# Graph network kernel: VectorE picks a gathered row by halving the candidates, with ScalarE copying the first half out of PSUM

## The chip, the cores and the metric

The kernel runs on one core of a Trainium2 chip. The metric is the device time of one execution in microseconds (us). Before the change three runs gave 5144.82, 5143.08 and 5143.58 us, median 5143.58.

## The reference, cut to what matters

```python
w = relu(edgefeats @ fnet_w1 + fnet_b1) @ fnet_w2 + fnet_b2      # 400000 edges, 13 -> 32 -> 256
W = w.reshape(-1, 16, 16)
for _ in range(2):                                               # NREPEATS
    xj = hx[edge_src]                                            # a row of 16 numbers for each edge
    m = einsum('ei,eio->eo', xj, W)
    agg = segment_sum(m, edge_dst, num_segments=12500) * inv_deg[:, None]
    hx = gru_cell(agg, hx, ...)
out = layernorm(x + hx)
```

The change concerns `hx[edge_src]`, the gather of 400000 rows out of a table of 12500, done twice. Everything else is as before.

## The kernel before, in words

The edges are sorted by destination. They are cut into tiles of 128 edges, one for each partition, and 64 tiles make a super-tile (a super, below). There are 49 supers (NSUP) in each of two rounds (`rnd` 0 and 1). Each super is worked in eight steps (`k`, HPS = 8) of eight tiles. Every engine runs its own program, written out by hand in its order, and meets the others at semaphores. A super has its number `s` in the round; `sup` counts through both rounds.

**Two ways to gather.** In each step of eight tiles POOL fetches five (six in step 0 of round 0) by indirect DMAs (line 535), and TensorE gathers the last three (two there) for the super that comes next. The numbers stand in BY_PE (line 33). POOL may be up to three steps ahead of the products (LEAD, line 532).

**The gather on TensorE.** The table is held in SBUF as `parts`: partition p and block kb hold 25 consecutive rows of 16 numbers (AR = 25, KB = 4), split into a high and a low part. ScalarE makes the one-hot matrix `src_hot` from the edges' block numbers: for each kb an absolute difference (`src_hots`, line 603), then one Relu over all four (line 607). TensorE multiplies it with the parts (`gather_rows`, line 722, 8 matmuls a tile, 24 for three tiles) into one of three PSUM banks `ps_g[j]`. After that each edge has 25 candidate rows, 400 numbers, in PSUM, of which one is its own.

**The pick on VectorE.** `rows_hot` (line 1125) writes once for each super `at_hot`, a one-hot of length 25 for each edge. `pick_rows` (line 1137) multiplies the 400 candidates of a tile by it, from PSUM into the SBUF tile `picked`, and raises `s_picked`, which frees the bank. `keep_rows` (line 1145) sums the 25 candidates of a step's tiles in one reduction of 1200 elements into `xg`, where the gathered rows of all tiles come together.

**The order of the work.** In step k of a super TensorE does `products` (line 732, 16 matmul records), in round 0 `hidden` for the next super (line 709), then what belongs to the step: in step 0 the `aggregate` of the super before (line 755, 32 records) behind some `own_sums` (line 745), in step 2 `turn` (line 762), in steps 4 and 5 `scatter` (line 776). At the end of the step stands `gather_rows` for step k of the next super. It waits for `s_src_hot` and for the pick of the tile that had the bank before (`slot_free`).

ScalarE in step 0 does `src_hots` of step 0 of the next super, `keep_agg` (line 582, waits for the aggregate), `keep_products` (line 576), in round 0 `relu` (line 570), and then `src_hots` of step 1. In steps 1 to 6 it begins with `src_hots` of step k + 1, which waits until the gather of step k - 1 is through, because there are two buffers of `src_hot`. Then come `keep_products` and `relu`. Step 7 has no `src_hots`.

VectorE in step k does `spread` (line 1092, the product of `xg` with the destination's one-hot, which TensorE's `products` of the same step waits for), `one_hot` and `keep_hot` (lines 1080 and 1100), in some steps `add_windows` (line 1165) and `keep_own` (lines 1115 and 1119), then the picks and the reduction for the gather of step k - 1, and once a super `places` (line 1151) and `rows_hot`.

## Time and profile before

| | us |
|---|---|
| median of three runs | 5143.58 |
| span of the profiled execution | 6694.6 |
| TensorE matmuls busy in it | 5648.0 (84%) |
| VectorE busy | 4296.9 (64%) |
| POOL busy | 3811.1 (57%) |
| ScalarE busy | 3179.0 (47%) |

The times are those of unrecorded runs; no time other than its span is given for the profiled execution, which is 1551 us longer than the median. The profile counts an instruction as busy from its start to its end, and neighbours on an engine may overlap. The ends of matmuls are modelled. Idle time stands with what ended it: "issue" where the profile shows nothing that was waited for, "remote" where the release came from something it can't name.

### The profile page before, as it was taken

To read this page: it belongs to the slowest core of one execution; us is meant where nothing else is said; L and a number is where in the kernel's file an instruction comes from. 1 tells how busy PE (TensorE), PEld (TensorE's weight loads), DVE (VectorE), ACT (ScalarE), POOL (GpSimd) and SP (SyncE) were. 2 spreads that over 40 slices of the span, in tenths; PEclk is the share of its full clock that TensorE was granted. 3 is DMA by queue.
4 is the path that set the end of the run, shared out by engine and by line. 5 is a ranking of instruction groups with operands and counts; after the bars stand their busy time and mean duration, and the time that the engine had idled before them with its cause. 6 is when DMAs were issued, how large, how long until landed. Compare 5 with 4: busy or idle time off the path is not lost.

```text
span 6694.6 us, 119595 instructions
## 1 busy us (share of the span) xinstructions
PE 5648.0 (84%) x38360; PEld 4666.6 (70%) x38361; DVE 4296.9 (64%) x7146; ACT 3179.0 (47%) x5259; POOL 3811.1 (57%) x4021
## 2 busy tenths in 40 slices
PE   2888888888888888888858888888888888888887
PEld 1777777777777777777647777776777777777775
DVE  3766666666666666666636666666666666666665
ACT  1554555445554545454325454454545454444442
POOL 6355555555555555555555555555555555555553
PEclk7988998889898999998878898898988889888887
DMA  4111111111111111111111111111111111111110
GB/s 107 46 34 48 34 48 34 48 34 48 34 48 44 39 48 34 48 34 48 25 47 29 40 29 40 33 37 39 31 40 29 40 29 41 29 40 29 40 29 20
DMA packets 197656, 263.32 MB, mean 39 GB/s; under 512 B 95745, under 2 KB 165942, under 8 KB 184205
## 3 DMA queue, kind: packets, MB, share of 16 engines
q1 hardware_dynamic: 61885, 216.66, 9.5%
q0 software_dynamic: 128192, 33.07, 4.8%
q10 hardware_dynamic: 7026, 6.21, 0.4%
q8 instruction: 348, 5.70, 0.4%
q14 instruction: 205, 1.68, 0.1%
HBM read 195.73 MB, written 54.92 MB: 37 GB/s over the span
## 4 chain that ended last, share of the span: by engine, by line
PE 65%; issue 14%; another core or an unknown queue 10%; ACT 6%; DVE 3%; DVEq 1%; DMA 0%; POOL 0%; ACTq 0%; POOLq 0%; SPq 0%
PE ps_all L722 45%; PE ps_all L732 8%; ACT src_hot L603 3%; PE ps_all L755 3%; PE ps_all L745 3%; PE ps_all L709 3%; PE ps_all L776 2%; ACT src_hot L607 2%; DVE shared L1137 1%; DVE fan L1092 1%; PE ps_all L762 0%; ACT shared L576 0%; ACT h_sb L570 0%; DVE xg L1145 0%
## 5 line engine op out<-in xcount | busy, mean ns | idle before, releaser
L722 PE MATMUL ps_all<-parts,src_hot 125*128 125x400 f32 x18048 | 3820.4, 368 | 258.7 <-issue 166.4
L722 PEld LDWEIGHTS ps_all<-parts,src_hot 125*128 125x128 f32 x18048 | 3501.9, 202 | 482.6 <-issue 367.7
L535 POOL DMA_INDIRECT xg<-in_x,idx x2027 | 1923.4, 949 | 1394.3 <-issue 556.1
L535 POOL DMA_INDIRECT xg<-h_rows,idx x1979 | 1873.1, 946 | 1371.6 <-issue 518.7
L1137 DVE TENSOR_TENSOR shared<-ps_all,at_hot 128x400 f32<-128x400 f32 x2256 | 1211.8, 566 | 1858.8 <-remote 1168.4
L603 ACT ACTIVATE src_hot<-keys,neg_key 128x384 fp32r<-128x384 int16 (+1 forms) x3072 | 1617.0, 599 | 1653.1 <-remote 979.0
L732 PE MATMUL ps_all<-fan,h_sb 128*32 128x160 f32 x12544 | 825.0, 316 | 489.5 <-issue 435.8
L1092 DVE TENSOR_TENSOR fan<-xg,ps_all 128x1280 f32<-128x1280 f32 x784 | 1158.8, 1478 | 88.0 <-DVE xg L1145 33.4
L607 ACT ACTIVATE src_hot<-src_hot 128x1536 fp32r<-128x1536 f32 (+1 forms) x768 | 1122.2, 1461 | 72.3 <-ACT src_hot L603 2.8
L1145 DVE TENSOR_REDUCE xg<-shared 128x48 f32<-128x1200 f32 (+1 forms) x768 | 1056.7, 1376 | 75.6 <-DVE shared L1137 1.0
L732 PEld LDWEIGHTS ps_all<-fan,h_sb 128*32 128x32 f32 x12544 | 391.8, 111 | 842.4 <-issue 794.9
L576 ACT COPY shared<-ps_all 128x320 f32<-128x320 f32 x784 | 330.2, 421 | 638.1 <-remote 431.2
L582 ACT COPY agg_sb<-ps_all 128x160 f32<-128x160 f32 x98 | 28.7, 293 | 981.0 <-remote 630.7
L755 PE MATMUL ps_all<-shared,w2s 128*64 128x160 f32 x3136 | 328.9, 349 | 70.3 <-issue 69.3
L745 PE MATMUL ps_all<-xg,shared 128*80 128x136 f32 (+1 forms) x1568 | 323.0, 317 | 75.1 <-issue 58.7
L709 PE MATMUL ps_all<-w_sb,ef 105*128 105x264 f32 x784 | 314.5, 483 | 66.5 <-issue 43.9
L745 PEld LDWEIGHTS ps_all<-xg,shared 128*80 128x80 f32 x1568 | 223.5, 168 | 193.1 <-issue 150.3
L755 PEld LDWEIGHTS ps_all<-shared,w2s 128*64 128x64 f32 x3136 | 259.3, 161 | 126.5 <-issue 117.6
L1165 DVE TENSOR_TENSOR acc_all<-acc_all,ps_all 33x144 f32 (+1 forms) x384 | 114.1, 297 | 236.3 <-remote 174.3
L709 PEld LDWEIGHTS ps_all<-w_sb,ef 105*128 105x128 f32 x784 | 131.0, 207 | 191.1 <-issue 179.4
L776 PE MATMUL ps_all<-place,agg_t 80*33 80x144 f32 (+1 forms) x1568 | 189.6, 336 | 64.0 <-issue 60.4
L1115 DVE TENSOR_TENSOR shared<-ps_all,mask 80x256 f32<-80x256 f32 (+3 forms) x490 | 180.4, 368 | 42.1 <-remote 20.4
(120 smaller groups left out, 1383.7 us busy)
## 6 DMA issues: line engine op xcount, KB each, us to landing
keys<-key_d SPq DMA_DIRECT2D x96, 768.0 KB
h_d<-h_sb SPq DMA_DIRECT2D x49, 1056.0 KB
h_sb<-h_d SPq DMA_DIRECT2D x49, 1056.0 KB
xg<-in_x,idx POOLq DMA_INDIRECT x2027
xg<-h_rows,idx POOLq DMA_INDIRECT x1979
ef<-in_ef_t SPq DMA_DIRECT2D x49, 420.0 KB
acc_all<-agg_t SPq DMA_DIRECT2D x1, 3161.0 KB
idx<-in_src_tiles SPq DMA_DIRECT2D x98, 32.0 KB
```

What stands on the lines that cost most here:

```text
L535: pool.indirect_dma_start(out=xg[:, buf, at, 0:C], out_offset=None, in_=rows_of, in_offset=bass.IndirectOffsetOnAxis(ap=idx[:, buf, at:at ...
L576: act.copy(pev[:, :, 2 * k:2 * k + 2, :].rearrange("p i u n -> p u i n"), ps_p[k % 2][:, 0:2 * C * WIN].rearrange("p (u i n) -> p u i n", ...
L603: act.activation(src_hot[:, k % 2, kb, 0:some * P], keys[:, buf, first * P:(first + some) * P], ACT.Abs, bias=neg_key[:, kb:kb + 1]).then_ ...
L607: act.activation(hot_of, hot_of.bitcast(F32), ACT.Relu, bias=1.0, scale=-1.0).then_inc(s_src_hot, some)
L709: pe.matmul(ps_h[:, 0:HT * HA], ef[:, buf, k, :], w1_sb[:], start=True, stop=True).then_inc(s_h, 1)
L722: last = pe.matmul(ps_g[j], src_hot[0:KP, k % 2, kb, j * P:(j + 1) * P], parts[0:KP, m, kb, :], start=(kb == 0 and m == 0), stop=(kb == KB ...
L732: last = pe.matmul(ps_p[k % 2][b * HID:(b + 1) * HID, u * C * WIN:(u + 1) * C * WIN], h_sb[:, buf, k * HT + u * BPS + b, 0:HID], fan[:, k ...
L745: last = pe.matmul(ps_own[n][:, u, 0:TQ * ca], hot_sb[:, j, b].rearrange("p t n -> p (t n)"), xg[:, buf].rearrange("p (j t b) c -> p j b t ...
L755: last = pe.matmul(ps_agg[lo:lo + BPS * C, 0:TPB * WIN], w2s[:, i, :], pev[:, i].rearrange("p t n -> p (t n)"), start=(i < 2), stop=(i >= ...
L1092: dve.tensor_tensor(fan[:, k % 2], xg[:, buf, k * HT:(k + 1) * HT, 0:C].unsqueeze(3).to_broadcast([P, HT, C, WIN]), hot[:, k % 2].unsqueez ...
L1137: dve.tensor_tensor(picked[:, j], ps_g[j].rearrange("p (a c) -> p c a", a=AR), at_hot[:, u].unsqueeze(1).to_broadcast([P, C, AR]), ALU.mul ...
L1145: dve.tensor_reduce(xg[:, buf, at:at + many, 0:C], picked[:, 0:many], AX_X, ALU.add).then_inc(s_xg_pe, many)
```

## The change

The 25 candidates are halved twice. NEAR is 13 and FEW is 7. ScalarE copies the first 13 candidates of a tile (208 numbers) from PSUM to the SBUF tile `near_rows`. VectorE overlays the other 12 (192 numbers) from PSUM by a predicated copy, in those edges whose row lies in the second half (`is_far[:, 0]`). It then overlays candidates 7 to 12 on 0 to 5 for a whole step's tiles (288 numbers), where `is_far[:, 1]` says so. It multiplies seven candidates by a one-hot of length 7 (336 numbers for three tiles) and sums them (336 numbers).

```diff
+NEAR = (AR + 1) // 2
+FEW = (NEAR + 1) // 2
...
+            def near_half(rnd, s, k):
+
+                wait_pos(act, s_cut, pe_count(rnd, s, pe_tiles(rnd, k)[0][0]))
+                for j, (n, _, _) in enumerate(pe_tiles(rnd, k)):
+                    act.wait_ge(s_g, pe_count(rnd, s, n) + 1)
+                    act.copy(near_rows[:, j].rearrange("p a c -> p (a c)"), ps_g[j][:, 0:NEAR * C]).then_inc(s_near, 1)
...
                     for k in range(HPS):
+                        if k > 0 and not is_last(i):
+                            near_half(rnd, 2 * i + par + 1, k - 1)
+                        elif k == 0 and not is_first(i, par):
+                            near_half(rnd, 2 * i + par, HPS - 1)
                         if k == 0 and not is_last(i):
                             src_hots(rnd, i + par, 1 - par, 2 * i + par + 1, 0)
...
             def rows_hot(rnd, s):
 
-                wait_pos(dve, s_picked, pe_count(rnd, s, 0))
-                dve.tensor_tensor(at_hot[:], iota_ps[:, 0:AR].unsqueeze(1).to_broadcast([P, TG, AR]),
-                                  at_pe[:, bass.ds(s * TG, TG)].unsqueeze(2).to_broadcast([P, TG, AR]),
+                mine = bass.ds(s * TG, TG)
+                wait_pos(dve, s_cut, pe_count(rnd, s, 0))
+                dve.tensor_tensor(at_hot[:], iota_ps[:, 0:FEW].unsqueeze(1).to_broadcast([P, TG, FEW]),
+                                  at_pe[:, mine].unsqueeze(2).to_broadcast([P, TG, FEW]),
                                   ALU.is_equal).then_inc(s_at_hot, 1)
+                dve.tensor_scalar(is_far[:, 0], at_side[:, mine], 2.0, None, ALU.is_ge).then_inc(s_at_hot, 1)
+                dve.wait_ge(s_at_hot, 3 * (rnd * (NSUP - 1) + s) - 1)
+                dve.scalar_tensor_tensor(out=is_far[:, 1], in0=is_far[:, 0], scalar=-2.0, in1=at_side[:, mine],
+                                         op0=ALU.mult, op1=ALU.add).then_inc(s_at_hot, 1)
...
                         if n == 0:
-                            dve.wait_ge(s_at_hot, rnd * (NSUP - 1) + s)
-                        dve.wait_ge(s_g, pe_count(rnd, s, n) + 1)
-                        wait_pos(dve, s_xg_pe, pe_count(rnd, s, n - j))
-                        dve.tensor_tensor(picked[:, j], ps_g[j].rearrange("p (a c) -> p c a", a=AR),
-                                          at_hot[:, u].unsqueeze(1).to_broadcast([P, C, AR]),
-                                          ALU.mult).then_inc(s_picked, 1)
+                            dve.wait_ge(s_at_hot, 3 * (rnd * (NSUP - 1) + s))
+                            dve.nop(nofuse=True)
+                        dve.wait_ge(s_near, pe_count(rnd, s, n) + 1)
+                        dve.nop(nofuse=True)
+                        dve.copy_predicated(near_rows[:, j, 0:AR - NEAR, :],
+                                            is_far[:, 0, u:u + 1].unsqueeze(2).to_broadcast([P, AR - NEAR, C]),
+                                            ps_g[j][:, NEAR * C:AR * C].rearrange("p (a c) -> p a c", c=C)).then_inc(
+                                                s_picked, 1)
...
             def keep_rows(rnd, s, buf, k):
...
                 dve.wait_ge(s_picked, pe_count(rnd, s, n) + many)
-                dve.tensor_reduce(xg[:, buf, at:at + many, 0:C], picked[:, 0:many], AX_X,
+                dve.nop(nofuse=True)
+                dve.copy_predicated(near_rows[:, 0:many, 0:NEAR - FEW, :],
+                                    is_far[:, 1, u:u + many].unsqueeze(2).unsqueeze(3).to_broadcast(
+                                        [P, many, NEAR - FEW, C]),
+                                    near_rows[:, 0:many, FEW:NEAR, :]).then_inc(s_few, many)
+                dve.wait_ge(s_few, pe_count(rnd, s, n) + many)
+                wait_pos(dve, s_xg_pe, pe_count(rnd, s, n))
+                dve.tensor_tensor(few_rows[:, 0:many], near_rows[:, 0:many, 0:FEW, :].rearrange("p m a c -> p m c a"),
+                                  at_hot[:, u:u + many].unsqueeze(2).to_broadcast([P, many, C, FEW]),
+                                  ALU.mult).then_inc(s_cut, many)
+                dve.wait_ge(s_cut, pe_count(rnd, s, n) + many)
+                dve.tensor_reduce(xg[:, buf, at:at + many, 0:C], few_rows[:, 0:many], AX_X,
                                   ALU.add).then_inc(s_xg_pe, many)
```

In the first super VectorE works out `at_pe` and the new `at_side` for all tiles once; four more small operations over 1176 columns and a drain are added there (`columns_of_tiles`).

On ScalarE the rows at the start of a super in round 0 (step 0, then the beginning of step 1) read so before; line 603 and 607 are `src_hots`, 582 `keep_agg`, 576 `keep_products`, 570 `relu`:

```order
L603 ACTIVATE src_hot<-keys,neg_key 128x256 [waits s_g,s_keys0]
L603 ACTIVATE src_hot<-keys,neg_key 128x256 x3
L607 ACTIVATE src_hot<-src_hot 128x4x256 [waits s_src_far]
L582 COPY agg_sb<-ps_all 128x160 [waits s_agg]
L576 COPY shared<-ps_all 128x2x16x10 [waits s_p]
L570 ACTIVATE h_sb<-ps_all 128x264 [waits s_h,s_h_out0]
L603 ACTIVATE src_hot<-keys,neg_key 128x384 [waits s_g]
L603 ACTIVATE src_hot<-keys,neg_key 128x384 x3
L607 ACTIVATE src_hot<-src_hot 128x1536 [waits s_src_far]
L603 ACTIVATE src_hot<-keys,neg_key 128x384 [waits s_g]
```

In the changed kernel the same stretch is these rows (line 611 and 615 are `src_hots`, 622 is the new copy of the near half; its lines are those of the changed kernel):

```order
L622 COPY shared<-ps_all 128x208 [waits s_g,s_cut]
L622 COPY shared<-ps_all 128x208 [waits s_g] x2
L611 ACTIVATE src_hot<-keys,neg_key 128x256 [waits s_g,s_keys0]
L611 ACTIVATE src_hot<-keys,neg_key 128x256 x3
L615 ACTIVATE src_hot<-src_hot 128x4x256 [waits s_src_far]
L590 COPY agg_sb<-ps_all 128x160 [waits s_agg]
L584 COPY shared<-ps_all 128x2x16x10 [waits s_p]
L578 ACTIVATE h_sb<-ps_all 128x264 [waits s_h,s_h_out0]
L611 ACTIVATE src_hot<-keys,neg_key 128x384 [waits s_g]
L611 ACTIVATE src_hot<-keys,neg_key 128x384 x3
L615 ACTIVATE src_hot<-src_hot 128x1536 [waits s_src_far]
L622 COPY shared<-ps_all 128x208 [waits s_g,s_cut]
L622 COPY shared<-ps_all 128x208 [waits s_g]
L611 ACTIVATE src_hot<-keys,neg_key 128x384 [waits s_g]
```

So three copies that wait for the gather of step 7 now stand ahead of the first `src_hots` of a super, and the copies of the gather of step 0 stand behind the `src_hots` of step 1.

On VectorE step 4 of a super read so before; the first three rows are `spread`, `one_hot` and `keep_hot`, the last two the picks and the reduction for the gather of step 3:

```order
L1092 TENSOR_TENSOR fan<-xg,ps_all 128x1280 [waits s_xg0_4,s_xg_pe,s_p,s_hot]
L1080 TENSOR_TENSOR ps_all<-ps_all,rel 128x80 [waits s_hot_sb]
L1100 COPY shared<-ps_all 128x2x4x10
L1137 TENSOR_TENSOR shared<-ps_all,at_hot 128x400 [waits s_xg_pe,s_g] x3
L1145 TENSOR_REDUCE xg<-shared 128x3x16 [waits s_picked]
```

Now they are:

```order
L1120 TENSOR_TENSOR fan<-xg,ps_all 128x1280 [waits s_xg0_4,s_xg_pe,s_p,s_hot]
L1108 TENSOR_TENSOR ps_all<-ps_all,rel 128x80 [waits s_hot_sb]
L1128 COPY shared<-ps_all 128x2x4x10
L1171 COPY_PREDICATED shared<-is_far,ps_all 128x192 [waits s_near] x3
L1181 COPY_PREDICATED shared<-is_far,shared 128x3x96 [waits s_picked]
L1187 TENSOR_TENSOR shared<-shared,at_hot 128x336 [waits s_xg_pe,s_few]
L1191 TENSOR_REDUCE xg<-shared 128x3x16 [waits s_cut]
```

The pick no longer waits for TensorE but for ScalarE's copy (`s_near`), and four operations became six, the last four of them in a chain.

## Rows read from the trace of the kernel before

**Rows 1.** The page: span, busy shares, and the chain that ended last by engine.
```profile
span 6694.6 us, 119595 instructions
...
PE 5648.0 (84%) x38360; PEld 4666.6 (70%) x38361; DVE 4296.9 (64%) x7146; ACT 3179.0 (47%) x5259; POOL 3811.1 (57%) x4021
...
PE 65%; issue 14%; another core or an unknown queue 10%; ACT 6%; DVE 3%; DVEq 1%; DMA 0%; POOL 0%; ACTq 0%; POOLq 0%; SPq 0%
```

**Rows 2.** Groups of matmuls: count | busy us, mean ns of one | idle before.
```profile
L722 PE MATMUL ps_all<-parts,src_hot 125*128 125x400 f32 x18048 | 3820.4, 368 | 258.7 <-issue 166.4 <-ACT src_hot L607 74.4 <-DVE shared L1137 11.0
...
L732 PE MATMUL ps_all<-fan,h_sb 128*32 128x160 f32 x12544 | 825.0, 316 | 489.5 <-issue 435.8 <-DVE fan L1092 48.6 <-ACT h_sb L570 2.8
...
L755 PE MATMUL ps_all<-shared,w2s 128*64 128x160 f32 x3136 | 328.9, 349 | 70.3 <-issue 69.3
L709 PE MATMUL ps_all<-w_sb,ef 105*128 105x264 f32 x784 | 314.5, 483 | 66.5 <-issue 43.9 <-DMA ef<-in_ef_t 18.8 <-ACT h_sb L570 2.4
...
L745 PE MATMUL ps_all<-xg,shared 128*80 128x136 f32 (+1 forms) x1568 | 323.0, 317 | 75.1 <-issue 58.7
```

**Rows 3.** The chain in order of time, 2236 to 2260: start, us, what.
```profile
2237.04 0.68 PE ps_all L732 x16
2237.72 0.64 PE ps_all L709 x2
2238.37 4.37 PE ps_all L722 x24
...
2244.06 0.47 PE ps_all L745 x4
...
2246.30 1.83 PE ps_all L755 x22
```

**Rows 4.** Busy time of each engine in a stretch; third from the right: granted clock.
```profile
2237.00:2249.00 12.00, 11.34 (x102) 9.55 (x102) 8.73 (x12) 4.21 (x11) 6.38 (x8) 1.00 0.55 182
```

**Rows 5.** Groups of VectorE and ScalarE.
```profile
L1137 DVE TENSOR_TENSOR shared<-ps_all,at_hot 128x400 f32<-128x400 f32 x2256 | 1211.8, 566 | 1858.8 <-remote 1168.4 <-PE ps_all L722 506.7 <-issue 180.3
...
L1145 DVE TENSOR_REDUCE xg<-shared 128x48 f32<-128x1200 f32 x720 | 1010.0, 1403 | 75.5 <-DVE shared L1137 1.0 <-issue 0.5
...
L576 ACT COPY shared<-ps_all 128x320 f32<-128x320 f32 x784 | 330.2, 421 | 638.1 <-remote 431.2 <-PE ps_all L732 179.2 <-issue 25.5
...
L1080 DVE TENSOR_TENSOR ps_all<-ps_all,rel 128x80 f32<-128x80 f32 x784 | 189.2, 241 | 0.2 <-issue 0.2
...
L582 ACT COPY agg_sb<-ps_all 128x160 f32<-128x160 f32 x98 | 28.7, 293 | 981.0 <-remote 630.7 <-PE ps_all L755 313.9 <-issue 36.4
```

**Rows 6.** Instructions in order of time, round 1, from a gather's end (start, us).
```profile
5027.67 0.57 DVE L1137 TENSOR_TENSOR shared<-ps_all,at_hot 128x400 f32<-128x400 f32 x1 [0.88 <-PE ps_all L722]
...
5028.35 1.40 DVE L1145 TENSOR_REDUCE xg<-shared 128x48 f32<-128x1200 f32 x1
...
5032.63 1.04 DVE L1137 TENSOR_TENSOR shared<-ps_all,at_hot 128x400 f32<-128x400 f32 x2
```

**Rows 7.** The same, round 0, from the end of an aggregate to the gather of step 1.
```profile
2248.17 0.29 ACT L582 COPY agg_sb<-ps_all 128x160 f32<-128x160 f32 x1 [6.22 <-PE ps_all L755]
...
2248.47 0.95 POOL L535 DMA_INDIRECT xg<-in_x,idx  x1 [0.30 <-issue]
...
2248.96 2.13 ACT L603 ACTIVATE src_hot<-keys,neg_key 128x384 fp32r<-128x384 int16 x4
...
2251.19 1.48 ACT L607 ACTIVATE src_hot<-src_hot 128x1536 fp32r<-128x1536 f32 x1
...
2252.72 1.72 PE L722 MATMUL ps_all<-parts,src_hot 125*128 125x400 f32 x8 [0.16 <-issue]
```

**Rows 8.** The same place in round 1.
```profile
3643.16 0.29 ACT L582 COPY agg_sb<-ps_all 128x160 f32<-128x160 f32 x1 [12.13 <-PE ps_all L755]
...
3645.90 1.49 ACT L607 ACTIVATE src_hot<-src_hot 128x1536 fp32r<-128x1536 f32 x1
...
3648.36 2.81 PE L722 MATMUL ps_all<-parts,src_hot 125*128 125x400 f32 x14
```

More of the change, by code:

```diff
@@ L175, in gnn_program @@
         near_tmp, far_tmp = (shared[:, lo:lo + CHUNK * TPB] for lo in (3920, 4120))
-        picked = shared[:, 4320:4320 + 3 * C * AR].rearrange("p (m c a) -> p m c a", m=3, a=AR)
+        near_rows = shared[:, 4320:4320 + 3 * C * NEAR].rearrange("p (m a c) -> p m a c", m=3, a=NEAR)
+        few_rows = shared[:, 4320 + 3 * C * NEAR:4320 + 3 * C * (NEAR + FEW)].rearrange("p (m c a) -> p m c a", m=3, a=FEW)
         agg_sb = sb("agg_sb", [P, TPB * WIN])
@@ L194, in gnn_program @@
         keys = sb("keys", [P, 2, TG * P], I16)
-        at_pe = sb("at_pe", [P, NSUP * TG])
+        at_pe = sb("at_pe", [P, NSUP * TG], I16)
         parts = sb("parts", [P, PARTS, KB, AR * C], F32R)
@@ L198, in gnn_program @@
         neg_key = sb("neg_key", [P, KB])
-        at_hot = sb("at_hot", [P, TG, AR])
+        at_hot = sb("at_hot", [P, TG, FEW])
+        at_side = sb("at_side", [P, NSUP * TG], I16)
+        is_far = sb("is_far", [P, 2, TG], U32)
         stat_all = sb("stat_all", [P, 2, GROUPS, RJ])
@@ L293, in gnn_program @@
         s_g = sem("s_g")
+        s_near = sem("s_near")
         s_picked = sem("s_picked")
+        s_few = sem("s_few")
+        s_cut = sem("s_cut")
         s_xg_pe = sem("s_xg_pe")
@@ L1050, in columns_of_tiles @@
                 key_of(key_col, src_col, whole_col)
-                dve.tensor_tensor(at_pe[:], src_col.bitcast(I32), key_col, ALU.subtract).then_inc(s_staged, 1)
+                link(dve.tensor_tensor(key_col, src_col.bitcast(I32), key_col, ALU.subtract))
+                link(dve.tensor_scalar(whole_col, key_col, float(NEAR) - 0.5, None, ALU.is_ge))
+                link(dve.scalar_tensor_tensor(out=key_col, in0=whole_col, scalar=-float(NEAR), in1=key_col,
+                                              op0=ALU.mult, op1=ALU.add))
+                link(dve.tensor_scalar(src_col, key_col, float(FEW) - 0.5, None, ALU.is_ge))
+                dve.scalar_tensor_tensor(out=at_side[:], in0=whole_col, scalar=2.0, in1=src_col,
+                                         op0=ALU.mult, op1=ALU.add)
+                dve.scalar_tensor_tensor(out=at_pe[:], in0=src_col, scalar=-float(FEW), in1=key_col,
+                                         op0=ALU.mult, op1=ALU.add)
+                dve.drain().then_inc(s_staged, 1)
                 dve.wait_ge(s_staged, 1)
```

6 lines of the change are left out of this document (3 added, 3 removed).

## The prediction

> **What bounds the kernel now.** I read the page first. TensorE is busy 84% of the recorded span, VectorE 64%, POOL 57%, ScalarE 47%, and the chain of work that ended last runs 65% through TensorE and 3% through VectorE [rows 1]. The reader is to see that the engine which the change relieves is hardly in that chain.
>
> A busy TensorE is not TensorE at its peak, so I next asked for the pieces of that chain in order of time, in a stretch whose granted clock is 1.00, the level of 2.4 GHz [rows 3, 4]. There 24 gather matmuls take 4.37 us, 16 records of products 0.68, two of hidden 0.64, four of own sums 0.47, and 22 of the aggregate 1.83, so 32 of them 2.66 [rows 3]. With the counts of the groups [rows 2]: 18048/24 = 752 gathers are 3286 us, 784 products 533, 392 hidden 251, 392 fours of own sums 184, 98 aggregates 261. That is 4515 us, 88% of the median of 5143.6. The other 628 us must hold the scatters, the turns, the head, the gate stages of two rounds and all stalls. So in unrecorded runs TensorE works nearly without a pause. The recorded span of 6694.6 is 1551 us longer; the idle time that the groups put down to "issue" and "remote" [rows 2, 5] is where it went, since the medians leave no room for it. I therefore count a change's cost in the stretches without stalls, add it to the recorded execution's own time and to the median alike, and trust no wait that stands as "remote".
>
> Then the picks. VectorE's 2256 picks had 1858.8 us of idle time before them, and none of that is VectorE's own work [rows 5]; in a clean step the pick of the third tile starts the moment the gather is over [rows 6]. The gather in turn waited for a pick only 11.0 us in all [rows 2]. VectorE follows TensorE; it doesn't hold it up.
>
> **The change, part by part.**
>
> *VectorE's work.* A line through 80 elements at 241 ns and 400 at 566 [rows 5] has 1.02 ns an element and 160 ns fixed. By it 192 elements are 355 ns, 288 are 452, 336 are 501. Before, three picks in a row start 0.47 apart (two take 1.04), then 0.11 of wait, then 1.40 of reduction: 2 x 0.47 + 0.57 + 0.11 + 1.40 = 3.02 us a step [rows 6]. Now it is 2 x 0.26 + 0.355 + 0.11 + 0.452 + 0.11 + 0.501 + 0.11 + 0.501 = 2.66. That is 0.36 less a step, 271 us over 752 steps. It is far less than the element count promises (1536 against 2400), because six fixed parts and four waits stand where there were four and two. From the third tile on nothing is won: 2.08 before, 2.14 now. None of this is on the path while TensorE is the bound, so I take 0 for it.
>
> The predicated copy stands nowhere in the trace. It can't be shorter than the row of 80 elements, 241 ns; if it needs two passes an element, 192 elements are 0.55 and 288 are 0.75, and a step gets 0.9 longer. I take one pass, as all VectorE rows here; both ends go into the range.
>
> The row shows 160 ns fixed in each VectorE instruction [rows 5]. The Trainium skill ("VectorE: DVE Perf Modes", section on the TRN2 errata) speaks against this change: sources in SBUF pay a fixed latency per instruction, so one should keep tiles at 512 elements or more, and here all four new kinds are below. Its table (120 cycles plus the elements from PSUM, 58 from SBUF, at 0.96 GHz) would make a step 0.78 shorter, where the rows make it 0.36; as neither is on the path, the forecast would be the same.
>
> *`rows_hot`.* 600 elements become 168 (by the line 0.77 and 0.33 us), and two operations of 24 elements with a wait come in (2 x 0.18 + 0.11): nothing. *`columns_of_tiles`* adds four operations of 1176 elements, 1.36 each, once, 5 us. They lie in the first super, where POOL fetches all 64 tiles at 1.25 us each (0.95 and 0.30 of issue [rows 7]), 80 us. I take 0; without that cover it would be 5.
>
> *ScalarE's work.* Copies of 160 and 320 numbers from PSUM take 293 and 421 ns [rows 5], so 208 take 331. 2256 of them are 747 us; ScalarE's 3179 become 3926, 76% of the median. The work fits, but the queue is in order, and its order decides at the start of each super.
>
> *Step 1, round 0.* Before, the gather of step 1 started at 2252.72, 0.05 after the one-hot of step 1 was ready (2251.19 + 1.48) [rows 7]: here ScalarE is already what TensorE waits for, last of all. Now the near halves of step 0 stand behind that one-hot, and the gather needs the bank of tile 0, which is free only after ScalarE's copy and VectorE's overlay. From the one-hot's end: 0.05 + 0.33, 0.10 until VectorE starts, 0.355, 0.05. That is 0.89 where it was 0.05, so 0.84 us more in each of 48 supers: **+40 us**.
>
> *Step 1, round 1.* The one-hot was ready at 3647.39 and the gather came only at 3648.36, since TensorE had more of its own to do [rows 8]. 0.89 later is 3648.28: it just fits, 0.
>
> *Step 0.* The three copies for step 7 now stand ahead of the first one-hot of a super. From the end of the gather of step 7: 0.05 + 0.33 + 0.05, then 3.71 for the one-hot (from 2248.96 to 2252.67 [rows 7]), 4.14 in all. TensorE meanwhile has products, own sums and aggregate, 0.68 + 0.47 + 2.66 = 3.81 [rows 3]. In round 1 the gather of step 0 so comes 0.33 to 0.39 late, and 0.39 x 48 = **+19 us**. In round 0 there is hidden too (0.64), and the one-hot is only two tiles wide: 0. Before, this one-hot was made while the gather of step 7 still ran.
>
> *Other steps.* ScalarE now has 3 x 0.33 + 3.71 + 0.42 + 0.38 + 0.1 = 5.6 in a step of round 0, TensorE 0.68 + 0.64 + 4.37 = 5.69; in round 1 it is 5.2 against 5.05. A backlog of 0.15 in a bare step is worked off in the steps with own sums, turn or scatter. I take 0. Queued behind the new waits for `s_g` are the one-hots, which waited for the same gather anyway.
>
> The sum is 40 + 19 = 59 us: 5143.6 + 59 = **5203 us** (the recorded span by the same sum 6754).
>
> **The rivals.**
>
> *VectorE does hold TensorE up in unrecorded runs*, in steps 5 to 7, where the window sums and own sums come on top and the fan is late. Then 0.36 is won in 3 steps of 96 supers, 104 us, and with the 59 the time is 5099. It decides once VectorE's slack in those steps is below the 0.36. For it: the sum of TensorE's pieces leaves some stalls open. Against it: 11.0 us of waits for picks [rows 2]. Chance 0.20.
>
> *POOL sets the pace.* 41 fetches at 1.25 us are 51 us a super, and 5143.6/98 is 52.5. Then a stall of 0.84 on TensorE falls into a wait that is there anyway, and nothing changes: 5144. Against it: the fetches' spacing would leave no room for the gate stages. Chance 0.15.
>
> *ScalarE becomes the bound.* If each copy costs 0.44, as the copies that wait for TensorE do (0.42 for 320 numbers), a step has 0.33 more, 0.2 over TensorE in round 0 and 0.45 in round 1, in the four steps that have nothing added: 48 x 4 x 0.65 = 125, and 5328. Chance 0.10.
>
> *The halving doesn't shorten VectorE's work*, because the predicated copy takes two passes: 0.9 - 0.36 = 0.54 more a step, late in three steps of eight: 96 x 3 x 0.54 = 156 and the 59 make 5358. Chance 0.05.
>
> **How the numbers follow.** My forecast has 0.50; with the last two slower is 0.65. A measurement of this kernel can tell about 0.2%, 10 us, from no change; the POOL case is the 0.15 for that, the VectorE case the 0.20 for faster. The range goes from 5085, a little under the VectorE case, to 5310, which takes in the forecast with half the backlog cost and leaves out most of the last two.
>
> **What would show it.** In the profile after: VectorE's busy time down by some 250 us and ScalarE's up by some 750; the predicated copies near 355 and 452 ns; in round 0 the gather of step 1 some 0.9 us behind the end of the one-hot of step 1 instead of 0.05; in round 1 the first gather of a super right behind its one-hot, which ends after the aggregate. Idle time before the gathers that is put down to VectorE's picks, 11.0 us now, should grow by tens of us. It is wrong if the time falls: then VectorE's work was on the path in unrecorded runs although the trace doesn't show it; or if nothing moves, then the start of a super has slack that I don't see.

## The result, and the profile after the change

Four runs of the changed kernel gave 5270.69 to 5279.98 us, median **5276.59**. Four runs of the kernel before beside them gave a median of 5144.20. The ratio is 1.0254, with a 95% interval from 1.0242 to 1.0266, so the change costs 132 us. The forecast was 59 us more, 5203, with a range up to 5310.

The recorded execution ahead of the prediction, and the first runs of the four kernels of experiments 4 to 6, fell where the kernel before takes 6.7 to 6.8 ms instead of 5.1 (there all four came out faster than it, at 0.986 to 0.993 of its time, even the two that only add work), and their times are not used. I ran the kernel before again, unchanged, to have its profile beside the others:

> The kernel before, unchanged, to have a second profile of it, since the first one's span was 1551 us above the median. All theories: 5144 us, and a span within a few us of it. The order theory (the new copies stand wrongly in ScalarE's queue at the start of a super) expects step 1 of round 0 near 5.85 us, against 6.87 in the changed kernel, and step 0 of round 1 near 8.0. The POOL theory (the new product on VectorE, with two inputs in SBUF, and POOL's fetches hold each other up) expects no fetch over 960 ns here, where the changed kernel has a tenth of them over 1050, and rounds of which POOL fills clearly less than in the changed kernel.

It gave 5145.53 us, ratio 1.0001 [0.9991, 1.0010], with a profiled span of 5147.8. The order theory missed its two figures: step 1 of round 0 takes 6.14 us here (5.85 expected), and step 0 of round 1 takes 8.79 on average (8.0 expected), as long as in the changed kernel (8.77). From here on "before" means this profile. These are its span and busy line, the chain that ended last by engine, and its groups of gathers, fetches, picks and reductions (count | busy us, mean ns of one | idle time before them):

```profile
span 5147.8 us, 119595 instructions
...
PE 4905.7 (95%) x38360; PEld 4260.6 (83%) x38361; DVE 4269.4 (83%) x7146; ACT 3171.3 (62%) x5259; POOL 3807.1 (74%) x4021
...
PE 62%; POOL 15%; issue 11%; DMA 4%; ACT 4%; DVE 3%; DVEq 1%; POOLq 0%; ACTq 0%; SPq 0%
...
L722 PE MATMUL ps_all<-parts,src_hot 125*128 125x400 f32 x18048 | 3504.6, 349 | 37.9 <-DVE shared L1137 17.6
...
L535 POOL DMA_INDIRECT xg<-in_x,idx x2027 | 1923.0, 949 | 621.3 <-issue 585.7
L535 POOL DMA_INDIRECT xg<-h_rows,idx x1979 | 1869.4, 945 | 614.1 <-issue 575.2
...
L1137 DVE TENSOR_TENSOR shared<-ps_all,at_hot 128x400 f32<-128x400 f32 x2256 | 1195.9, 564 | 314.3 <-PE ps_all L722 301.7
...
L1145 DVE TENSOR_REDUCE xg<-shared 128x48 f32<-128x1200 f32 (+1 forms) x768 | 1056.6, 1376 | 75.6 <-DVE shared L1137 1.4
```

The same lines of the changed kernel:

```profile
span 5276.6 us, 127115 instructions
...
PE 4929.8 (93%) x38360; PEld 4279.2 (81%) x38361; DVE 4058.2 (77%) x8879; ACT 3754.4 (71%) x7515; POOL 3932.2 (75%) x4021
...
PE 51%; POOL 20%; issue 13%; DMA 6%; DVE 4%; ACT 3%; DVEq 1%; POOLq 0%; ACTq 0%; SPq 0%
...
L741 PE MATMUL ps_all<-parts,src_hot 125*128 125x400 f32 x18048 | 3518.0, 350 | 60.5 <-DVE shared L1171 51.4
...
L543 POOL DMA_INDIRECT xg<-in_x,idx x2027 | 1990.2, 982 | 626.6 <-issue 586.1
L543 POOL DMA_INDIRECT xg<-h_rows,idx x1979 | 1927.3, 974 | 614.3 <-issue 574.4
...
L622 ACT COPY shared<-ps_all 128x208 f32<-128x208 f32 x2256 | 711.7, 334 | 1070.2 <-PE ps_all L741 986.1
...
L1171 DVE COPY_PREDICATED shared<-is_far,ps_all 128x192 f32<-128x192 uint32 x2256 | 719.7, 366 | 327.6 <-ACT shared L622 320.0
...
L1187 DVE TENSOR_TENSOR shared<-shared,at_hot 128x336 f32<-128x336 f32 (+1 forms) x768 | 569.5, 742 | 76.1 <-DVE shared L1181 10.8
L1191 DVE TENSOR_REDUCE xg<-shared 128x48 f32<-128x336 f32 (+1 forms) x768 | 380.6, 496 | 80.3 <-DVE shared L1187 1.4
L1181 DVE COPY_PREDICATED shared<-is_far,shared 128x288 f32<-128x288 uint32 (+1 forms) x768 | 371.2, 483 | 77.9 <-DVE shared L1171 4.7
```

TensorE does the same work in the same time (+24 us), and VectorE does 211 us less. What grew is POOL's fetches, of which nothing was changed: 949 and 945 ns each became 982 and 974. Their 33 x 2027 + 29 x 1979 ns are 124 us, nearly the whole loss of 132.

**What a fetch costs only counts where POOL sets the pace, and it does.** Before each fetch stand some 0.30 us of "issue" (1161 us over 4006), so a fetch comes every 1.25 us. The table of 1000 us stretches shows it, the first in round 0 and the second in round 1 (columns: PE, PEld, DVE, ACT and POOL busy, each with its count of instructions, then the granted clock). Before:

```profile
1000.00:2000.00 1000.00, 990.38 (x7710) 862.98 (x7709) 832.72 (x1388) 648.86 (x1130) 756.10 (x801) 1.00 0.22 52
3500.00:4500.00 1000.00, 968.30 (x7766) 854.31 (x7762) 863.91 (x1442) 638.75 (x1000) 756.25 (x801) 1.00 0.20 46
```

After:

```profile
1000.00:2000.00 1000.00, 971.82 (x7531) 847.17 (x7530) 771.54 (x1692) 747.50 (x1541) 761.93 (x782) 0.99 0.21 52
3500.00:4500.00 1000.00, 948.88 (x7552) 833.11 (x7551) 795.68 (x1754) 741.06 (x1442) 762.01 (x782) 0.99 0.18 44
```

Before, 801 fetches go into 1000 us in both rounds. 1000/801 is 1.248 us each, without a gap, although TensorE is 99% busy in the one round and 97% in the other. All 4006 fetches at 1.25 us are 5007 us, and only 140 us of the span are left for the head, the gate stages and the tail. These need no more: in the trace 62 us without a fetch lie between the rounds and 67 behind the last fetch. After the change 782 fetches fit in (1.279 us each): 2.4% fewer, for a time 2.5% longer. Counted over all fetches from start to start, the kernel before spends 17 us beyond 1.248 each and the changed kernel 147. These 130 us are the whole difference of the two spans (129). Two engines are nearly equal here: in round 0 TensorE has 1% of slack beside POOL, in round 1 3%.

**What makes a fetch slow** is to be seen in the order of time (start, us, what):

```profile
2241.80 0.94 POOL L543 DMA_INDIRECT xg<-in_x,idx  x1 [0.31 <-issue]
...
2242.28 0.49 DVE L1181 COPY_PREDICATED shared<-is_far,shared 128x288 f32<-128x288 uint32 x1
2242.86 0.76 DVE L1187 TENSOR_TENSOR shared<-shared,at_hot 128x336 f32<-128x336 f32 x1
2243.05 1.34 POOL L543 DMA_INDIRECT xg<-in_x,idx  x1 [0.30 <-issue]
2243.73 0.51 DVE L1191 TENSOR_REDUCE xg<-shared 128x48 f32<-128x336 f32 x1
...
2244.70 0.94 POOL L543 DMA_INDIRECT xg<-in_x,idx  x1 [0.30 <-issue]
```

The fetch that lies beside the halving's product (line 1187) takes 1.34 us where its neighbours take 0.94. Of the 4006 fetches 469 took over 1.00 us, and 445 of these overlap with such a product; before there were 22 over 1.00. The product is the one that reads both its inputs from SBUF. The pick before it, line 1137, had one in PSUM.

It also matters which of the two begins first. In the piece the product was running when the slow fetch began, and the fetch ends 0.77 us behind the product's end. So it is in general: 318 of the 445 began under such a product and end 0.76 to 0.79 us after it; of the other 127, 116 began under the predicated copy of line 1181, which reads two inputs from SBUF as well. The first fetch of the piece had begun before either and took 0.94. By this a longer product costs twice: it meets more starts of fetches, and holds each up for longer.

The second SBUF input gave the theory: **a VectorE instruction with two inputs in SBUF holds up POOL's fetch**. The rivals were that the order of ScalarE's queue costs the time (the mechanism of the forecast), and that VectorE's chain of four instructions does.

The Trainium skill ("SBUF — State Buffer", in "SBUF: two separate sides") says that VectorE and GpSimd share a pair of ports as an exclusive lock, which an operation of VectorE with two SBUF inputs takes, "only against a GpSimd op that reads SBUF". The runs here agree with it in direction for an indirect fetch, which the Trainium skill doesn't name there (445 of 469 slow fetches beside such a product; experiments 2, 4 and 6 take the second SBUF input away). That a port is what is held no trace shows, and the fetch shows little of a lock in the other direction: the product takes 742 ns with both inputs in SBUF and 741 with one (experiment 2). I had not used this for the prediction.

### The profile page after: what moved, and what is told of

The parts are those of the page before. It is cut to its first block, busy times and chain, and to the rows that moved or that the text cites. A ratio compares the mean times of both kernels' runs of the same rounds, so it can differ in the third digit from the quotient of the medians.

```text
span 5276.6 us, 127115 instructions
## 1 busy us (share of the span) xinstructions
PE 4929.8 (93%) x38360; PEld 4279.2 (81%) x38361; DVE 4058.2 (77%) x8879; ACT 3754.4 (71%) x7515; POOL 3932.2 (75%) x4021
## 4 chain that ended last, share of the span: by engine, by line
PE 51%; POOL 20%; issue 13%; DMA 6%; DVE 4%; ACT 3%; DVEq 1%; POOLq 0%; ACTq 0%; SPq 0%
PE ps_all L741 35%; POOL xg L543 20%; PE ps_all L751 6%; DMA xg<-h_rows,idx 4%; PE ps_all L728 4%; PE ps_all L764 2%; PE ps_all L774 2%; DVE fan L1120 2%; ACT src_hot L611 2%; DMA xg<-in_x,idx 2%; PE ps_all L795 1%; DVE shared L1171 1%; ACT shared L622 0%; DVE shared L1187 0%; DVEq L1206 0%
## 5 line engine op out<-in xcount | busy, mean ns | idle before, releaser
L741 PE MATMUL ps_all<-parts,src_hot 125*128 125x400 f32 x18048 | 3518.0, 350 | 60.5 <-DVE shared L1171 51.4
L741 PEld LDWEIGHTS ps_all<-parts,src_hot 125*128 125x128 f32 x18048 | 3270.3, 189 | 192.7 <-issue 127.3
L622 ACT COPY shared<-ps_all 128x208 f32<-128x208 f32 x2256 | 711.7, 334 | 1070.2 <-PE ps_all L741 986.1
L1171 DVE COPY_PREDICATED shared<-is_far,ps_all 128x192 f32<-128x192 uint32 x2256 | 719.7, 366 | 327.6 <-ACT shared L622 320.0
L751 PE MATMUL ps_all<-fan,h_sb 128*32 128x160 f32 x12544 | 602.0, 310 | 212.5 <-DVE fan L1120 204.8
L1187 DVE TENSOR_TENSOR shared<-shared,at_hot 128x336 f32<-128x336 f32 (+1 forms) x768 | 569.5, 742 | 76.1 <-DVE shared L1181 10.8
L1191 DVE TENSOR_REDUCE xg<-shared 128x48 f32<-128x336 f32 (+1 forms) x768 | 380.6, 496 | 80.3 <-DVE shared L1187 1.4
L1181 DVE COPY_PREDICATED shared<-is_far,shared 128x288 f32<-128x288 uint32 (+1 forms) x768 | 371.2, 483 | 77.9 <-DVE shared L1171 4.7
L774 PE MATMUL ps_all<-shared,w2s 128*64 128x160 f32 x3136 | 245.4, 311 | 0.7 <-issue 0.7
L1147 DVE TENSOR_REDUCE agg_t<-shared 80x32 f32<-80x256 f32 (+3 forms) x490 | 181.0, 369 | 16.9
```

Of the source, the lines that this page charges most:

```text
L622: act.copy(near_rows[:, j].rearrange("p a c -> p (a c)"), ps_g[j][:, 0:NEAR * C]).then_inc(s_near, 1)
L741: last = pe.matmul(ps_g[j], src_hot[0:KP, k % 2, kb, j * P:(j + 1) * P], parts[0:KP, m, kb, :], start=(kb == 0 and m == 0), stop=(kb == KB ...
L751: last = pe.matmul(ps_p[k % 2][b * HID:(b + 1) * HID, u * C * WIN:(u + 1) * C * WIN], h_sb[:, buf, k * HT + u * BPS + b, 0:HID], fan[:, k ...
L774: last = pe.matmul(ps_agg[lo:lo + BPS * C, 0:TPB * WIN], w2s[:, i, :], pev[:, i].rearrange("p t n -> p (t n)"), start=(i < 2), stop=(i >= ...
L1171: dve.copy_predicated(near_rows[:, j, 0:AR - NEAR, :], is_far[:, 0, u:u + 1].unsqueeze(2).to_broadcast([P, AR - NEAR, C]), ps_g[j][:, NEAR ...
L1187: dve.tensor_tensor(few_rows[:, 0:many], near_rows[:, 0:many, 0:FEW, :].rearrange("p m a c -> p m c a"), at_hot[:, u:u + many].unsqueeze(2 ...
```

## The experiments

**1. The order of ScalarE's queue, undone alone.** The near copies of step 0 are issued between the absolute differences and the Relu of step 1's one-hot. The loss was looked for in round 0, but the edit does it in both rounds.

```diff
                for kb in range(KB):
...
+                if between is not None:
+                    between()
...
-                        if k > 0 and not is_last(i):
+                        if k > 1 and not is_last(i):
                             near_half(rnd, 2 * i + par + 1, k - 1)
...
-                            src_hots(rnd, i + par, 1 - par, 2 * i + par + 1, 1)
+                            src_hots(rnd, i + par, 1 - par, 2 * i + par + 1, 1,
+                                     lambda: near_half(rnd, 2 * i + par + 1, 0))
```

> The changed kernel, with ScalarE's two or three near copies of step 0 moved ahead of the Relu of the one-hot of step 1 (they stood behind it). Order theory: the gather of step 1 in round 0 no longer waits 1.0 us, 48 x 1.0 = 48 us less, 5229 us, with half of the loss gone. POOL theory: round 1 keeps its 51.2 us a super, since POOL sets it, and round 0 falls only as far as POOL lets it, to 41 fetches at 1.26 = 51.7; at most 5245. If VectorE's slow product is the cause: no change, 5277.

Measured: 5273.92 us, ratio 1.0253 [1.0236, 1.0270], no gain. The mean length of step 1 in round 0 did fall from 6.80 to 6.46 us (6.14 before the change), but step 0 grew from 7.84 to 8.16. In round 1, where nothing was to be mended, step 1 grew from 5.31 to 6.10, and the super did not get longer (51.21 and 51.07). The fetches stayed at 982 and 973 ns, and with them the time. While POOL sets the pace, a stall removed from TensorE turns up as a wait for rows in the next step.

**2. One input of the product moved to PSUM.** `at_hot` goes into the free part of bank 7, and nothing else changes.

```diff
-        at_hot = sb("at_hot", [P, TG, FEW])
...
+        at_hot = ps_all[:, 7 * BANK + SPAN + 2 * HT * WIN:7 * BANK + SPAN + 2 * HT * WIN + TG * FEW].rearrange(
+            "p (u a) -> p u a", a=FEW)
```

> The changed kernel, with the one-hot of seven (at_hot) in PSUM instead of SBUF, so that VectorE's product has only one input in SBUF. POOL theory: the fetches are all back at 941 to 955 ns, round 1 gains what POOL lost, some 0.6 us a super or 30 us, 5245. Order theory: round 0 keeps its 1.0 us in step 1, no change, 5277. Slow-product theory: if two SBUF inputs are what makes it 754 instead of 501 ns, it falls to 501 and the time with it; if its strided reading is, it stays at 754.

Measured: **5193.68 us, ratio 1.0094 [1.0077, 1.0111]**. 83 of the 132 us are gone by the place of one small operand, more than the POOL theory had expected (5245), which had counted some 30 us in round 1 alone: by the profiles round 0 is 34 us shorter and round 1 51. Its groups of fetches and its product:

```profile
L544 POOL DMA_INDIRECT xg<-in_x,idx x2027 | 1942.5, 958 | 639.5 <-issue 584.7 <-PE ps_all L752 53.9 <-DMA idx<-in_src_tiles 0.9
L544 POOL DMA_INDIRECT xg<-h_rows,idx x1979 | 1877.1, 948 | 614.1 <-issue 569.0 <-PE ps_all L752 33.8 <-DMA h_rows<-shared 11.3
...
L1188 DVE TENSOR_TENSOR shared<-shared,ps_all 128x336 f32<-128x336 f32 (+1 forms) x768 | 569.0, 741 | 76.1 <-DVE shared L1182 10.8
```

The product takes what it took, 741 ns, so it is not VectorE's time that was won. 162 fetches still take over 1.00 us, 140 of them beside the second predicated copy.

**3. The product reads in order and writes in steps**, to see why it takes 742 ns where I had worked out 501, and what a shorter one would give.

```diff
-                dve.tensor_tensor(few_rows[:, 0:many], near_rows[:, 0:many, 0:FEW, :].rearrange("p m a c -> p m c a"),
-                                  at_hot[:, u:u + many].unsqueeze(2).to_broadcast([P, many, C, FEW]),
+                dve.tensor_tensor(few_rows[:, 0:many].rearrange("p m c a -> p m a c"), near_rows[:, 0:many, 0:FEW, :],
+                                  at_hot[:, u:u + many].unsqueeze(3).to_broadcast([P, many, FEW, C]),
```

> The changed kernel, with VectorE's product running over the candidates in the order in which they lie in SBUF (it reads densely and writes with a stride, before it read with a stride and wrote densely). If strided reading makes the product slow, it falls from 754 to near 501 ns, 0.25 us a step. Slow-product theory: 752 steps x up to 0.25 us on the path of round 1 gives up to 90 us, 5190. Order theory: 5277, as the start of a super doesn't depend on it by more than 0.1 us. POOL theory: less time with the port held, some us at most, 5270.

Measured: a miss. The product takes 796 ns, the time is 5254.83 us, ratio 1.0211 [1.0194, 1.0228], and the fetches 974 ns in both rounds. The product was not shorter, so the run tells nothing about a shorter one. The small gain of 22 us against the changed kernel goes with the fetches again: in round 0 their mean fell from 982 to 974 ns, 16 us over 2027 of them, and the two profiled spans lie 15 us apart. Why the fetches of round 0 met the longer product less often, no run shows.

**4. The masks in PSUM too.** The second predicated copy (line 1181) reads data and mask from SBUF, so it was suspected for the slow fetches that were left. (In the first runs of this and the next three kernels the fetches came out alike: 951 ns in round 0 for this kernel, 948 for the next, 955 and 947 for the two of experiment 6.)

```diff
-        is_far = sb("is_far", [P, 2, TG], U32)
+        far_sb = sb("far_sb", [P, TG], U32)
...
+        is_far = [far_sb, ps_all[:, far_at:far_at + TG].bitcast(U32)]
```

> The changed kernel with the halving's product reading one input from PSUM, and the second predicated copy's mask in PSUM as well, so that no VectorE instruction of the pick reads two inputs from SBUF. Read beside the earlier version with the product alone moved (5193.7 us). Theory (VectorE instructions with two SBUF inputs hold up POOL's fetches): no fetch is slow any more, mean 945 to 950 ns, and the time falls to about 5170 us; what is left over the kernel before is the later start of step 1's gather in round 0. Rival (the rest of the loss is that order alone, and the second predicated copy has no part in it): 5194 us, as with the product alone moved.

Measured: 5191.90 us, ratio 1.0072 [1.0055, 1.0088]. The fetches are 948 and 944 ns and 23 take over 1.00 us, as many as before the change. The time fell less than expected (5170), and its interval overlaps with that of experiment 2. The reason stands in the order of time, at the start of a super in round 0:

```profile
2210.88 1.48 ACT L618 ACTIVATE src_hot<-src_hot 128x1536 fp32r<-128x1536 f32 x1
2212.27 0.55 ACT L625 COPY shared<-ps_all 128x208 f32<-128x208 f32 x2
2212.68 0.64 DVE L1174 COPY_PREDICATED shared<-far_sb,ps_all 128x192 f32<-128x192 uint32 x2 [3.86 <-ACT shared L625]
...
2213.20 4.61 PE L744 MATMUL ps_all<-parts,src_hot 125*128 125x400 f32 x24 [0.95 <-DVE shared L1174]
```

The one-hot is ready at 2212.36 and the gather starts at 2213.20, 0.84 later. In the kernel before, it starts right behind the one-hot:

```profile
2220.37 1.48 ACT L607 ACTIVATE src_hot<-src_hot 128x1536 fp32r<-128x1536 f32 x1
...
2221.91 4.64 PE L722 MATMUL ps_all<-parts,src_hot 125*128 125x400 f32 x24 [0.17 <-ACT src_hot L607]
```

With POOL free, the wait of the forecast is real and on the path: step 1 of round 0 is 6.87 us against 6.14 (medians), a super of round 0 51.98 against 51.10, one of round 1 49.94 against 49.99 (means). 0.88 x 48 is 42 us, and 0.72% of 5155 is 37.

**5. Masks in PSUM and the order undone.**

> The same as the version with product and masks in PSUM, and the near copies of step 0 issued ahead of the Relu of step 1's one-hot in round 0. Theory (POOL's fetches, 1.25 us apart, pace both rounds once nothing holds them up): about 5146 us, within 10 of the kernel before, although VectorE has 200 us less to do. Rival (TensorE bounds and VectorE's saved time shows once the order is mended): 5100 us or less.

Measured: **5169.10 us, ratio 1.0025 [1.0015, 1.0035]**. The edit of experiment 1, worth nothing there, is worth 23 us here (5191.90 to 5169.10). By the profiles round 0 is 24 us shorter, and round 1 4 us longer: there the edit makes step 1 6.30 us instead of 5.32, most of which lies under POOL's pace. A version with the edit in round 0 alone was not run. The last 0.25% are in round 0: beside the twin of experiment 6, which ran on the same chip, round 0 is 10 us longer and round 1 no longer, and step 1 of round 0 takes 6.43 where it took 6.14, 0.29 x 48 = 14 us. The theory's "within 10 of the kernel before" is missed by 4 us (5155.23 beside it). The rival (5100 or less) is out. VectorE's lighter load shows nowhere, though it is busy 50 us less in each stretch (columns as above):

```profile
1000.00:2000.00 1000.00, 983.31 (x7648) 856.52 (x7647) 782.94 (x1718) 760.73 (x1570) 750.00 (x793) 1.00 0.22 53
3500.00:4500.00 1000.00, 959.15 (x7697) 848.21 (x7696) 817.02 (x1785) 752.83 (x1468) 756.06 (x801) 1.00 0.19 46
```

In round 1 801 fetches pass again, POOL's full pace; in round 0, where TensorE is 98% busy, it is 793.

**6. The second SBUF input alone.** The kernel before gets one VectorE product of 256 elements per step, whose output nothing uses; in the twin one of its inputs is in PSUM.

```diff
+                dve.tensor_tensor(prod_x[:].rearrange("p (h o) i -> p h (o i)", h=2),
+                                  ident[:].unsqueeze(1).to_broadcast([P, 2, P]),
+                                  iota[:, 0:P].unsqueeze(1).to_broadcast([P, 2, P]), ALU.mult)
```

> The kernel before with one VectorE product of two SBUF inputs (128 x 256 elements, its output used by nothing) added in each step, and nothing else changed. Theory (such a product holds up POOL's fetches): the fetches' mean goes from 947 to 955 ns or more, some of them over 1.1 us, and the time is 5160 to 5215 us. Rival (VectorE's extra time in a step is what costs): the same time as its twin with one input in PSUM.

> The twin of the port test: the kernel before with the same added VectorE product per step, 128 x 256 elements, one of its inputs in PSUM. Theory: no fetch is slow (mean 944 to 948 ns), and the time is that of the kernel before within 15 us (5145 to 5160), since VectorE's work lies beside POOL's pace. Rival (VectorE's time is what costs): as slow as the version with both inputs in SBUF, 5160 us or more.

Measured: 5181.49 us, ratio 1.0050 [1.0034, 1.0067], with both inputs in SBUF, and 5160.91, ratio 1.0007 [0.9997, 1.0017], for the twin. The product, line 1147, and the fetches of round 0, first with both in SBUF:

```profile
L535 POOL DMA_INDIRECT xg<-in_x,idx x2027 | 1938.2, 956 | 626.1 <-issue 585.6 <-PE ps_all L732 39.5 <-DMA idx<-in_src_tiles 0.9
...
L1147 DVE TENSOR_TENSOR prod_x<-ident,iota 128x256 f32<-128x256 f32 x768 | 320.9, 418 | 0.0
```

Then the twin:

```profile
L535 POOL DMA_INDIRECT xg<-in_x,idx x2027 | 1924.8, 950 | 627.7 <-issue 587.7 <-PE ps_all L732 39.0 <-DMA idx<-in_src_tiles 0.9
...
L1147 DVE TENSOR_TENSOR prod_x<-ident,ps_all 128x256 f32<-128x256 f32 x768 | 315.2, 410 | 0.0
```

The same work in the same time on VectorE, 410 and 418 ns: in PSUM it costs nothing that can be told, from SBUF it costs 21 us more than the twin. 137 fetches against 18 take over 1.00 us, 116 of the 137 beside that product. This is the theory without the change, and it is shown. (The twin lies 1 us above the 5160 of its expectation, on a chip where the kernel before takes 5155.23.) Here too the start decides: of the 103 fetches that began under the product with at least 0.25 us of it still to come 87 took over 1.00 us, and 5 of the 492 in which it began 0.1 to 0.9 us behind their start.

**7. Product in PSUM and order undone, mask left in SBUF.**

> The near copies early and the product's one-hot in PSUM, the second predicated copy's mask left in SBUF. Beside the version with that mask in PSUM too (1.0025 times the kernel before). Theory (the predicated copy with data and mask in SBUF holds up fetches as the product does): some fetches over 1.1 us in both rounds (mean 950 to 958 ns), and 1.004 to 1.007. Rival (it has no part): 1.0025, and no fetch slow.

Measured: 5177.58 us, ratio 1.0065 [1.0048, 1.0081]. 136 fetches take over 1.00 us, 113 of them beside the second predicated copy, which takes 489 ns. With the mask in PSUM the ratio was 1.0025 and 23 fetches were slow. The predicated copy has its part, some 20 us by this pair (its twin ran on another chip, where the kernel before takes 10 us more, so this goes by ratios) and 11 us by the step from experiment 2 to 4 (1.0094 to 1.0072). Of the 537 fetches in which the predicated copy began 0.1 to 0.9 us behind their start none was slow.

**8. Why 336 elements take 742 ns.** Four products of 196 elements that differ only in how they go through memory, added to the kernel of experiment 5:

```diff
+                dve.tensor_tensor(shape_x[:, 0].rearrange("p (m c a) -> p m c a", m=2, c=14),
+                                  ident[:, 0:112].rearrange("p (a c) -> p c a", c=16)[:, 0:14].unsqueeze(1).to_broadcast([P, 2, 14, 7]),
+                                  iota[:, 0:14].rearrange("p (m a) -> p m a", m=2).unsqueeze(2).to_broadcast([P, 2, 14, 7]), ALU.mult)
...
```

> The version with product, masks in PSUM and near copies early, with four VectorE products of 128 x 196 elements added in each step, outputs used by nothing. They differ in access alone: (1) one input from SBUF in steps of 16 elements, as the kernel's product reads; (2) everything read and written in order; (3) read in order, written in steps of 7; (4) as 1 from PSUM. By the rate of the other VectorE rows (one element per 1.04 ns and some 150 ns) each would take about 357 ns. Theory (reading or writing SBUF in steps costs): 1 and 3 about 500 ns, 2 and 4 about 357. Rival (the length of the inner run, 7, costs): 1, 2 and 4 about 500, 3 about 357. Only the durations are read, not the time of the kernel.

In the order of the expectation the lines are 1200, 1203, 1206 and 1209 (groups by shape, columns as before):

```profile
L1206 DVE TENSOR_TENSOR shape_x<-ident,iota 128x196 f32<-128x196 f32 x768 | 416.8, 543 | 0.0
L1200 DVE TENSOR_TENSOR shape_x<-ident,iota 128x196 f32<-128x196 f32 x768 | 378.6, 493 | 0.0
...
L1209 DVE TENSOR_TENSOR shape_x<-ps_all,iota 128x196 f32<-128x196 f32 x768 | 288.1, 375 | 0.0
L1203 DVE TENSOR_TENSOR shape_x<-ident,iota 128x196 f32<-128x196 f32 x768 | 271.8, 354 | 0.0
```

In order 354 ns, as the line through the other rows says. Read from SBUF in steps of 16 elements 493, written in steps of 7 elements 543, read from PSUM in steps of 16 only 375. So it is the steps in SBUF, not the short inner run (the 354 has it too) and not the two inputs. At 0.71 ns an element the steps are 239 ns for the product's 336, and it was 253 longer than worked out. It also tells why experiment 3 missed: it took the steps from the input and gave them to the output.

The Trainium skill ("SBUF — State Buffer", "Specifications (TRN2)") says that SBUF is read in lines of 16 bytes and wants at least two hits in each for full bandwidth. In steps of 64 bytes there is one, and the trace agrees in direction: 0.71 ns more an element from SBUF, 0.11 from PSUM.

**9. The layout turned.** In the kernel of experiment 5 the near rows are kept in the order in which the product reads them.

```diff
-        near_rows = shared[:, 4320:4320 + 3 * C * NEAR].rearrange("p (m a c) -> p m a c", m=3, a=NEAR)
+        near_rows = shared[:, 4320:4320 + 3 * C * NEAR].rearrange("p (m c a) -> p m a c", m=3, a=NEAR)
...
-                    act.copy(near_rows[:, j].rearrange("p a c -> p (a c)"), ps_g[j][:, 0:NEAR * C])
+                    act.copy(near_rows[:, j], ps_g[j][:, 0:NEAR * C].rearrange("p (a c) -> p a c", c=C))
```

> The version with product, masks in PSUM and near copies early, and the near rows kept in the order that the product reads (ScalarE's copy and the predicated copies write in steps of 13 elements, the product reads runs of 7 in order). Theory (reading SBUF in steps costs the product some 250 ns): the product falls from 754 to about 500 ns; ScalarE's copy stays at about 334 ns. Rival (the inner run's length costs): it stays at 754. The time is that of the version it is made from, 1.0025 times the kernel before, within 0.2%, since POOL's and TensorE's paces set it.

Measured: 6596.88 us, ratio 1.2822 [1.2801, 1.2843]. The product behaves as expected, the rest does not:

```profile
L1177 DVE COPY_PREDICATED shared<-far_sb,ps_all 128x192 f32<-128x192 uint32 x2256 | 2117.5, 1169 | 24.2 <-ACT shared L627 22.0 <-issue 0.7
...
L1187 DVE COPY_PREDICATED shared<-ps_all,shared 128x288 f32<-128x288 uint32 x720 | 1094.6, 1520 | 77.9 <-DVE shared L1177 4.7
L1193 DVE TENSOR_TENSOR shared<-shared,ps_all 128x336 f32<-128x336 f32 x720 | 363.3, 505 | 71.7 <-DVE shared L1187 10.8
```

The product takes 505 ns, within 4 of the 501 of the forecast. The expectation held for nothing else: the time was to be that of experiment 5 and ScalarE's copy 334 ns. The predicated copies now write in steps of 13 elements and went from 367 to 1169 ns and from 487 to 1520 (this one reads in such steps too), and ScalarE's copy went from 334 to 550. VectorE is busy 91% of the span and is the bound.

## Why the prediction was right or wrong

**The sign was right, and by a wrong account of the path.** The forecast of 59 us lost was made for a kernel that TensorE bounds. 132 were lost, by something the prediction does not have. That 5276.6 still lies under the range's end of 5310 is luck: that end was set with half the cost of a backlog on ScalarE, not with anything of POOL's.

**The step that failed: the dismissal of POOL as what sets the pace, and with it the 0 for VectorE's new instructions.** That "TensorE works nearly without a pause" is true (4905.7 us, 95% of the undisturbed span), but it does not make TensorE the only bound: POOL hardly pauses either (17 us beyond its pace in all). That rival was set aside with "the fetches' spacing would leave no room for the gate stages". That was worked out from 52.5 us a super, the median over 98, which already has the head and gate stages in it. 4006 fetches at 1.25 us are 5007 us and leave 136 of the median for them, and those stages need no more (62 us between the rounds, 67 at the end). The row for the 1.25 was there [rows 7]. The recorded execution hid the rest: with 1551 us of stalls in it, POOL was busy 57% and stood with 0% in the chain [rows 1], where the undisturbed one has 74% and 15%. Its own time showed that it was not the kernel as measured. I corrected the durations for that and not the question of who waits for whom. What the runs showed in its place: POOL issues a fetch every 1.248 us through both rounds, the change makes that 1.279, and 130 us are lost there.

**The rival itself was half right.** It had the bound, but concluded "nothing changes", because it took a fetch's 0.95 us as given. The change lengthened that to 0.98 on average.

**"None of this is on the path, I take 0 for it" failed in the other direction.** VectorE's saved time was indeed worth nothing: experiment 5 has it and is not faster than before. But VectorE's new instructions cost through POOL. The product alone was 83 us (1.0254 to 1.0094), the mask of the second predicated copy 11 (1.0094 to 1.0072) to 20 (1.0065 to 1.0025), in sum 94 to 103 of the 132. No price of an instruction on its own engine holds this.

**The order term was right in size, and its cause is shown for the larger part.** I had 0.84 us in step 1 of round 0, 40 us. With the fetches undisturbed the step is 0.73 longer, the super 0.88, 42 us. Undoing the order took 24 us of round 0 away (experiment 5); the rest was not taken away by any run. In the changed kernel most of it is hidden under POOL's slower pace, which is why undoing it there gave nothing. The 19 us for step 0 of round 1 did not come: with the fetches undisturbed a super of round 1 takes 49.94 us against 49.99. There POOL's 40 fetches take 50.0, so 0.39 us of delay would fall into slack; whether the delay was there was not looked at. The condition of the POOL rival held for that round.

**VectorE's saving was 0.07 us a step, not 0.36.** The predicated copies came near the line (366 and, for 288 elements, 491 ns for 355 and 452), and so did the reduction (503 at 336 elements for 501). The product did not: 754 for 501. By the groups, picks and reductions were busy 2252.5 us and are now 2041.0, but the idle time ahead of the last three kinds grew from 75.6 to 234.3. That leaves 53 us over the 768 steps (720 of three tiles, 48 of two; the forecast's 752 took all as three). The mis-sized term is reading SBUF in steps.

**The other rivals.** ScalarE as the bound is out: the copy takes 334 ns (331 forecast), and ScalarE is busy 71%. Two passes for a predicated copy are out by 366 ns. VectorE holding TensorE up is out: 17.6 us of waits for picks, and no gain in experiment 5.

What stays open is the last 0.25% of experiment 5 in round 0, which lies in the order of ScalarE's queue around step 1 by its place but which no run took away, and why the fetches of round 0 were shorter in experiment 3. No version was found that beats the kernel before. With POOL at 801 fetches per 1000 us and TensorE at 99% in round 0, less work on VectorE alone should not give one; that is argued from these counts.

## What to carry to other kernels

Before costing an edit, count the steady events of every engine per unit of time in an undisturbed stretch. An engine that is busy 74% can be the one that sets the pace when a fixed gap goes with each of its instructions. When work is moved from PSUM to SBUF, ask who else uses SBUF at that moment: here a VectorE instruction with two SBUF inputs slowed the indirect fetches on POOL, and putting a 168-element operand into PSUM gave 83 us back. When a layout is chosen, price the steps on both sides: for the shapes here steps cost least in reads from PSUM, and most in a predicated copy's writes to SBUF.

## What the runs showed of the hardware that I had not expected

- An indirect fetch on POOL of 0.944 us takes up to 1.34 in the piece shown when a VectorE product with two SBUF inputs runs beside it, and is not touched by one with an input in PSUM (experiment 6, 256 elements: 137 against 18 slow fetches of 4006).
- The fetch is held up by an instruction that was running when it began: it then ends 0.76 to 0.79 us behind the product's end (318 fetches of the changed kernel). An instruction that begins 0.1 to 0.9 us into a fetch leaves it alone (none slow of 537 in experiment 7, 5 of 492 in experiment 6).
- A predicated copy of 192 elements takes 366 ns when it writes SBUF in order and 1169 in steps of 13 elements, 4.2 ns more an element. A product pays 0.71 ns an element for reading in steps of 16 and 0.96 for writing in steps of 7; from PSUM, reading in steps costs 0.11.
- ScalarE's copy of 208 elements goes from 334 to 550 ns with the same steps in its output.
